# A windowed-attention and gated-FFN stream on one core: another hand-written order for all four engine queues, with other PSUM banks

## The chip, the cores and the metric

The kernel runs on one core of a Trainium2 chip. The metric is the time on the device in microseconds (us). In the rows PE is TensorE, DVE VectorE, ACT ScalarE, POOL GpSimd and SP SyncE; PEld are the weight loads of TensorE, which run beside its matmuls.

## The reference

Eight sequences of 256 tokens and 128 channels. First a layer norm modulated by a small conditioning vector, then causal attention with 8 heads of 128 (stage A), and the same modulation again. Then six layers, each a local attention and a gated FFN, both with a residual. Cut to what matters:

```python
for i in range(6):
    x = attn_layer(shift_tokens(x), Wqkv[i], ...) + x
    x = ffn_layer(shift_tokens(x), ...) + x

def shift_tokens(t):                 # second half of the channels comes from the token before
    a, s = jnp.split(t, 2, -1)
    return concat([a, pad(s, one token in front)[:-1]])

def attn_layer(x):                   # 16 heads of 64
    q, k, v = split(x @ Wqkv)        # 128 -> 3 * 1024
    q, k = l2norm(q) * qs, l2norm(k) * ks
    q, k = rotary(q) * scale, rotary(k) / scale
    sim = q . k * 8, windows of 32 queries on 64 keys, masked
    return softmax(sim) . v @ Wo     # 1024 -> 128

def ffn_layer(x):
    a, gate = split(layernorm(x) @ W1 + b1)      # 128 -> 2 * 341
    return a * gelu(gate) @ W2 + b2              # 341 -> 128
```

## The kernel before

**Work and slots.** A pair of sequences is the unit of the stream: four pairs, six layers, so 24 slots. Slot 0 is in the join (`join_pe`, `join_act`, `join_dve`, `join_pool`), where it overlaps the last sequence of stage A. The other 23 are written once as `pair_pe`, `pair_act`, `pair_dve` and `pair_pool` and called with the layer `l` and the pair `p`. After them `remainder` calls them twice more for the work left (the tail). With `c = 2 * p`, a slot holds three pairs at different ages:

- pair p: sequence c through the local attention up to its values, and the first half of sequence c+1;
- pair p-1: the rest of the attention of sequence c-1, and the output projection of c-2 and c-1;
- pair p-2: its FFN.

The conditions `on(p)`, `on(p - 1)`, `on(p - 2)` switch these off at the ends. In the last slot of a layer (`last(p)`) the projection weights of the next layer are also split into a high and a low part, six times each: the high parts by ACT (`split_high`), the low parts by DVE and POOL (`split_low`).

**The chain of one sequence.** `xt_turn` (PE transposes the input with a column shift), `xt_high` (ACT) and `xt_low` (DVE, L1379), then twelve `proj` (PE, L1428, each three matmuls of 512 columns). Eight of them are queries and keys: `square` (ACT, L1436), `square_sum`, `rotate_cos`, `rotate_sin` (DVE, L1447, L1463, L1468), `rotate_add` (POOL, L1472), nine `norm_step` for all eight, `normalise` (POOL, L1513, writes `qn`), `turn` (PE, four transposes through the helper at L336), `turn_copy` (ACT). Four are values: `move_v` (ACT, L1442). Then `mask` (ACT, writes the mask into a score bank), `scores` (PE, L1555), `row_max`, `less_max` (DVE), `exponent` (ACT, L1577), `row_sum`, `row_inverse` (DVE), `soft_norm` (POOL, L1590, on `sp`), `turn_p` (PE, L336), `copy_p` (ACT, L1608), `values` (PE, L1624), `copy_o` (ACT, L1634), `out_proj` (PE, L1644), `out_add` (DVE).

**The FFN of one pair.** Three transfers on SP's queue (`l_shift`, L1670 to L1683) bring the shifted rows after the pair's last `out_add`. `l_first` (ACT, L1689) copies the unshifted half and waits for their landing; then `l_stats`, `l_moments` (DVE), `l_root` (POOL, four small instructions: L314, L316, L1716, L1718), `l_norm` (ACT), `l_turn` (PE), `l_scale` (ACT), `hidden_gate`, `hidden_a` (PE), `gelu` (ACT), `gated` (DVE), `second_layer` (PE, L1751 to 1791 with `m_add` on DVE).

**What sets the order.** Each engine's queue is written out by hand as a list of calls, and an engine runs its list strictly in order. Every call waits by itself for its inputs. The banks are in constant tables; where a bank is used again, the list has an explicit wait for its last reader in front of the call:

```python
            if on(p - 1):
                e.wait_ge(b_ev.sem, b_ev.at(l * B + c - 1, 2))
                turn(e, l, c - 1, 0)
```

Here `b_ev` counts the value copies `move_v` of a sequence (0 to 3), `b_oc` its `copy_o`, `b_ab` its `rotate_sin`, `b_tc` its `turn_copy`, `b_sub` its `less_max`, `b_pc` its `copy_p`, `b_wx` its `out_add`. In the tables the first list is for even sequences and the second for odd ones. In the names of the rows, `pO`, `pQ` and the like are the eight PSUM banks, `sp` the softmax tiles, `ra`, `rb`, `rs` those of the rotation and the norms.

## Time and profile before

| | |
|---|---|
| median of 3 runs | 1841.77 us (1838.03 to 1850.27) |
| the profiled execution | 1840.85 us |
| its span | 1839.0 us |
| instructions | 65209 |
| PE busy in the span | 1685.9 us |

The span goes from the first instruction to the last; the profiled execution lasts 1.85 us more. Durations below are of this one execution. A matmul's recorded length contains its passage through the array, so consecutive matmuls overlap in the records. Idle time is written in brackets after the instruction that it precedes, with what released it.

### The profile page before, as it was taken

Reading aid. Unit: us, or ns where it says so; the run is one execution under the profiler, and the core shown is the slowest. Engines: PE = TensorE matmul, PEld = TensorE weight load, DVE = VectorE, ACT = ScalarE, POOL = GpSimd, SP = SyncE. Lnnn points to the kernel's source line nnn. Section 1 sums busy time; section 2 is a strip of 40 time slices with the busy share of each in tenths; the row PEclk is TensorE's granted clock in tenths of the full one; section 3 lists DMA queues with packets and bytes.
Section 4 is the critical chain, followed back from the end, with each engine's and each line's share of the span. In section 5 each row is a group of like instructions: output and inputs, shape, how many; then the busy total and the mean of one; then the engine's idle time right before and its main releaser. Section 6 shows DMA issues by size and latency. Waiting matters only on the chain. (4 is left out here: it accounts for less than half of the span.)

```text
span 1839.0 us, 65209 instructions
## 1 busy us (share of the span) xinstructions
PE 1685.9 (92%) x26499; PEld 1384.8 (75%) x26499; DVE 1541.4 (84%) x3101; ACT 1426.3 (78%) x2822; POOL 1395.0 (76%) x1566
## 2 busy tenths in 40 slices
PE   6999976899999999899999899998999989999985
PEld 4788865778778877787787688877877877887773
DVE  5878758788989898899899788988898988888962
ACT  3676764788888888888888788888888878887872
POOL 3777767878878888878787778887787878787850
PEclk9999998999999999999999999999999999999998
DMA  5000010111021201211110212012111111120111
GB/s 165 1 1 2 1 38 21 38 32 48 22 75 50 60 23 38 75 50 40 42 39 28 69 50 59 23 38 75 50 41 42 38 29 42 40 60 28 36 34 29
DMA packets 49368, 76.85 MB, mean 42 GB/s; under 512 B 16316, under 2 KB 29768, under 8 KB 49072
## 3 DMA queue, kind: packets, MB, share of 16 engines
q1 hardware_dynamic: 47600, 70.60, 13.2%
q8 instruction: 212, 3.47, 0.8%
q10 hardware_dynamic: 1472, 2.10, 0.3%
q14 instruction: 84, 0.69, 0.1%
HBM read 21.33 MB, written 1.05 MB: 12 GB/s over the span
## 5 line engine op out<-in xcount | busy, mean ns | idle before, releaser
L1472 POOL TENSOR_TENSOR ra<-ra,rb 128x512 f32<-128x512 f32 x384 | 492.6, 1290 | 89.8 <-DVE rb L1468 89.6
L1513 POOL TENSOR_TENSOR qn<-ra,rs 128x512 f32<-128x512 f32 x384 | 399.6, 1060 | 48.2 <-DVE rs L1506 48.2
L1447 DVE TENSOR_REDUCE ss<-sq 128x8 f32<-128x512 f32 x384 | 259.4, 675 | 71.7 <-ACT sq L1436 67.9
L1590 POOL TENSOR_TENSOR sp<-sp,rl 128x512 f32<-128x512 f32 x192 | 202.1, 1053 | 108.3 <-DVE rl L1585 107.1
L1577 ACT ACTIVATE sp<-sp 128x512 f32<-128x512 f32 x192 | 121.6, 634 | 52.2 <-DVE sp L1572 51.3
L1581 DVE TENSOR_REDUCE sm<-sp 128x8 f32<-128x512 f32 x192 | 128.3, 668 | 5.4 <-ACT sp L1577 5.4
L1608 ACT COPY pt<-pS 64x512 f32<-64x512 f32 x144 | 83.3, 579 | 53.8 <-PE pS L336 52.4
L1555 PE MATMUL pQ<-kT,qT 64*32 64x64 f32 x4608 | 111.3, 226 | 11.6 <-issue 7.7
L1468 DVE TENSOR_TENSOR rb<-pQ,rope 128x512 f32<-128x512 f32 x168 | 114.4, 681 | 1.1
L1463 DVE TENSOR_TENSOR ra<-pQ,rope 128x512 f32<-128x512 f32 x168 | 113.2, 674 | 0.6 <-POOL qn L1513 0.6
L1436 ACT ACTIVATE sq<-pQ 128x512 f32<-128x512 f32 x168 | 100.3, 597 | 15.7 <-PE pQ L1428 11.6
L1555 PEld LDWEIGHTS pQ<-kT,qT 64*32 64x32 f32 x4608 | 94.5, 105 | 18.0 <-issue 16.7
L1608 ACT COPY pt<-pM 64x512 f32<-64x512 f32 x144 | 83.8, 582 | 29.5 <-PE pM L336 28.7
L488 POOL TENSOR_TENSOR ra<-ra,rb 128x512 f32<-128x512 f32 x64 | 81.6, 1291 | 30.0 <-DVE rb L484 30.0
L1644 PE MATMUL pO<-woB,early 128*128 128x128 f32 x768 | 95.7, 278 | 3.3 <-issue 2.4
L1644 PE MATMUL pO<-woB,oT 128*128 128x128 f32 x768 | 95.8, 278 | 3.1 <-issue 3.0
L1644 PEld LDWEIGHTS pO<-woB,oT 128*128 128x128 f32 x768 | 91.8, 194 | 7.8 <-issue 4.5
L1428 PE MATMUL pQ<-w_high,xsh 128*128 128x512 f32 x192 | 92.5, 482 | 2.8 <-issue 2.8
L1644 PEld LDWEIGHTS pO<-woB,early 128*128 128x128 f32 x768 | 91.2, 194 | 3.9 <-issue 2.9
L554 POOL TENSOR_TENSOR sp<-sp,rl 128x128 f32<-128x128 f32 (+1 forms) x128 | 66.8, 545 | 34.8 <-DVE rl L548 34.7
L336 PE MATMUL pS<-eye,qn 128*128 128x128 f32 x480 | 75.7, 281 | 13.1 <-POOL qn L1513 6.1
L1751 PE MATMUL pP<-early,w 128*128 128x512 f32 x144 | 77.8, 622 | 3.1 <-ACT early L1743 2.1
(340 smaller groups left out, 5889.3 us busy)
## 6 DMA issues: line engine op xcount, KB each, us to landing
vs<-v SPq DMA_DIRECT2D x96, 384.0 KB, 3.3
wqkvA<-in_L_ffn_Wqkv SPq DMA_DIRECT2D x18, 512.0 KB, 5.0
vs<-v SPq DMA_DIRECT2D x96, 64.0 KB, 3.0
fx<-xr SPq DMA_DIRECT2D x24, 224.0 KB
woB<-in_L_ffn_Wo SPq DMA_DIRECT2D x6, 512.0 KB, 4.2
w<-in_L_ffn_W SPq DMA_DIRECT2D x6, 341.0 KB, 3.0
out<-x SPq DMA_DIRECT2D x4, 256.0 KB, 2.6
x<-in_L_attn_x SPq DMA_DIRECT2D x1, 768.0 KB, 8.2
```

The lines of the kernel that those rows point to most:

```text
L1436: e.activation(sq[:, j % 2, :], banks[PROJ_BANK[c % 2][n]], ACT.Square).then_inc(b_sq.sem, 1)
L1447: e.tensor_reduce(ss[:, j, :], sq[:, j % 2, :].rearrange("p (h d) -> p h d", d=DB), AX.X, ALU.add).then_inc(b_ss.sem, 1)
L1463: e.tensor_tensor(halves(ra[:, j, :]), r, w, ALU.mult)
L1468: e.tensor_tensor(halves(rb[:, j % 2, :]), r[:, :, ::-1, :], w, ALU.mult).then_inc(b_ab.sem, 1)
L1472: e.tensor_tensor(ra[:, j, :], ra[:, j, :], rb[:, j % 2, :], ALU.add).then_inc(b_ad.sem, 1)
L1513: e.tensor_tensor(qn[:, j % 4, :].rearrange("p (h d) -> p h d", d=DB), ra[:, j, :].rearrange("p (h d) -> p h d", d=DB), rs[:, c % 2, 8 * j ...
L1555: i = e.matmul(o[h][WIN * j:WIN * j + WIN, lo:lo + 2 * WIN], qT[g][r, k, WIN * w:WIN * w + WIN], kT[g][r, k, WIN * w:WIN * w + 2 * WIN], s ...
L1577: e.activation(sp[:, u, :], sp[:, u, :], ACT.Exp, scale=8.0).then_inc(b_ex.sem, 1)
L1581: e.tensor_reduce(sm[:, u, :], groups(sp[:, u, :]), AX.X, ALU.add).then_inc(b_sm.sem, 1)
L1590: e.tensor_tensor(y, y, rl[:, u, :].unsqueeze(2).to_broadcast([P, 8, 64]), ALU.mult).then_inc(b_pn.sem, 1)
L1608: i = e.copy(pt[r, g, u % 2, :, a, :], src[r, :, :])
L1644: i = e.matmul(o[:, t * M:(t + 1) * M], oT[c % 2][:, k, t * P:(t + 1) * P], woB[:, k, :], start=(k == 0), stop=(k == PAIRS - 1))
```

## The change

The four lists of the stream, and the four of the join, get another order, and the bank tables other numbers; the explicit waits in front of the calls follow from these. No call is added or removed, and SP's program, with the shift's transfers, is the same. The order comes from a search in which the shift's transfer was given a later landing. The core of the diff (the first lines are the bank tables; then the join of PE, ACT, DVE and POOL; then the lists of the stream in the same order):

```diff
@@ -50,18 +50,18 @@
...

-PROJ_BANK = [[6, 1, 7, 3, 1, 4, 5, 7, 3, 2, 5, 3], [1, 0, 1, 4, 7, 5, 1, 0, 2, 0, 5, 3]]
-TURN_BANK = [[0, 4, 7, 2, 1, 6, 4, 2], [5, 3, 0, 5, 2, 6, 5, 0]]
-SCORE_BANK = [[0, 2, 3, 2], [4, 0, 5, 0]]
-TURNP_BANK = [[4, 4, 6, 4], [7, 7, 7, 6]]
-VALUE_BANK = [[1, 3, 6, 2], [3, 7, 7, 6]]
+PROJ_BANK = [[4, 3, 2, 7, 1, 4, 3, 0, 2, 5, 3, 5], [0, 7, 1, 2, 7, 5, 6, 0, 4, 3, 2, 4]]
+TURN_BANK = [[6, 2, 4, 0, 6, 1, 1, 2], [4, 5, 1, 6, 4, 3, 5, 6]]
+SCORE_BANK = [[4, 0, 3, 4], [5, 0, 3, 0]]
+TURNP_BANK = [[2, 6, 0, 2], [7, 7, 6, 0]]
+VALUE_BANK = [[6, 1, 0, 6], [2, 7, 6, 1]]
 SCORE_BANKS = range(6)
-XT_FIRST = [2, 7]
-XT_BANK = [6, 7]
+XT_FIRST = [4, 1]
+XT_BANK = [7, 6]
 OUT_BANK = [6, 6]
-LTURN_BANK, Y_BANK = 2, 3
-GATE_BANK = [0, 6, 5]
-A_BANK = [2, 2, 2]
+LTURN_BANK, Y_BANK = 6, 1
+GATE_BANK = [6, 2, 7]
+A_BANK = [5, 6, 6]


 class Tally:
@@ -973,121 +973,121 @@
...
             a_values(e, 7, 2)
+            e.wait_ge(a_ex.sem, a_ex.at(7, 5))
+            xt_turn(e, 0, 0)
...
+            e.wait_ge(a_pc.sem, a_pc.at(7, 6))
+            proj(e, 0, 0, 1)
+            e.wait_ge(a_pj.sem, a_pj.at(7, 2))
             e.wait_ge(a_ex.sem, a_ex.at(7, 7))
...
-            e.wait_ge(a_pc.sem, a_pc.at(7, 6))
             proj(e, 0, 0, 3)
             e.wait_ge(a_pj.sem, a_pj.at(7, 5))
...
+            proj(e, 0, 1, 0)
+            e.wait_ge(b_ab.sem, b_ab.at(0, 3))
+            proj(e, 0, 1, 1)
+            e.wait_ge(a_y.sem, a_y.at(7, 0))
+            turn(e, 0, 0, 0)
             e.wait_ge(b_ab.sem, b_ab.at(0, 6))
-            proj(e, 0, 0, 11)
+            turn(e, 0, 0, 1)
             e.wait_ge(b_ev.sem, b_ev.at(0, 0))
-            proj(e, 0, 1, 0)
-            e.wait_ge(a_pc.sem, a_pc.at(7, 5))
-            turn(e, 0, 0, 0)
-            e.wait_ge(b_ev.sem, b_ev.at(0, 1))
-            turn(e, 0, 0, 1)
-            e.wait_ge(b_tc.sem, b_tc.at(0, 0))
-            proj(e, 0, 1, 1)
-            e.wait_ge(b_ab.sem, b_ab.at(0, 5))
-            turn(e, 0, 0, 2)
-            e.wait_ge(b_ab.sem, b_ab.at(1, 0))
             proj(e, 0, 1, 2)
...
@@ -1104,21 +1104,21 @@
...
+            e.wait_ge(a_pj.sem, a_pj.at(6, 11))
+            xt_high(e, 0, 0)
             a_exp(e, 7, 6)
             a_copy_p(e, 7, 4)
             e.wait_ge(a_ex.sem, a_ex.at(7, 3))
             a_mask(e, 7, 7)
             a_copy_p(e, 7, 5)
-            a_exp(e, 7, 7)
-            a_copy_p(e, 7, 6)
-            e.wait_ge(a_pj.sem, a_pj.at(6, 11))
-            xt_high(e, 0, 0)
-            a_copy_p(e, 7, 7)
             e.wait_ge(a_pj.sem, a_pj.at(7, 11))
             xt_high(e, 0, 1)
...
@@ -1186,19 +1184,16 @@
             a_max(e, 7, 6)
             a_inverse(e, 7, 5)
             a_gates(e, 7)
+            xt_low(e, 0, 0)
             a_inverse(e, 7, 6)
+            xt_low(e, 0, 1)
             a_max(e, 7, 7)
-            a_inverse(e, 7, 7)
-            xt_low(e, 0, 0)
-            a_residual(e, 7)
-            a_stats2(e, 7)
-            xt_low(e, 0, 1)
             square_sum(e, 0, 0, 0)
-            a_norm2(e, 7)
             e.wait_ge(a_tr.sem, a_tr.at(7, 0))
             rotate_cos(e, 0, 0, 0)
             e.wait_ge(a_ad.sem, a_ad.at(7, 6))
             rotate_sin(e, 0, 0, 0)
+            a_inverse(e, 7, 7)
             square_sum(e, 0, 0, 1)
...
@@ -1207,11 +1202,14 @@
             square_sum(e, 0, 0, 2)
             e.wait_ge(a_tr.sem, a_tr.at(7, 2))
             rotate_cos(e, 0, 0, 2)
+            a_residual(e, 7)
             rotate_sin(e, 0, 0, 2)
+            a_stats2(e, 7)
             square_sum(e, 0, 0, 3)
             e.wait_ge(a_tr.sem, a_tr.at(7, 3))
...
             a_soft(e, 7, 6)
+            rotate_add(e, 0, 0, 0)
             a_soft(e, 7, 7)
-            a_root2(e, 7)
-            a_modulate2(e, 7)
-            rotate_add(e, 0, 0, 0)
             rotate_add(e, 0, 0, 1)
             rotate_add(e, 0, 0, 2)
+            a_root2(e, 7)
             rotate_add(e, 0, 0, 3)
+            a_modulate2(e, 7)
             rotate_add(e, 0, 0, 4)
             rotate_add(e, 0, 0, 5)
             norm_step(e, 0, 0, 0)
...
@@ -1805,275 +1799,315 @@
...
             c = 2 * p
             if on(p - 1):
-                e.wait_ge(b_oc.sem, b_oc.at(l * B + c - 2, 2))
+                e.wait_ge(b_ev.sem, b_ev.at(l * B + c - 1, 0))
             if on(p):
                 xt_turn(e, l, c)
             if on(p - 1):
+                e.wait_ge(b_ev.sem, b_ev.at(l * B + c - 1, 3))
+                turn(e, l, c - 1, 0)
+                e.wait_ge(b_oc.sem, b_oc.at(l * B + c - 2, 3))
+            if on(p):
+                xt_turn(e, l, c + 1)
+            if on(p - 1):
+                e.wait_ge(b_ev.sem, b_ev.at(l * B + c - 1, 1))
+                turn(e, l, c - 1, 1)
+                e.wait_ge(b_oc.sem, b_oc.at(l * B + c - 2, 1))
+                turn(e, l, c - 1, 2)
+                e.wait_ge(b_tc.sem, b_tc.at(l * B + c - 1, 0))
+            if on(p):
+                proj(e, l, c, 0)
+            if on(p - 1):
+                e.wait_ge(b_ab.sem, b_ab.at(l * B + c - 1, 7))
+            if on(p):
+                proj(e, l, c, 1)
+            if on(p - 1):
                 e.wait_ge(b_ev.sem, b_ev.at(l * B + c - 1, 2))
-                turn(e, l, c - 1, 0)
-                e.wait_ge(b_ev.sem, b_ev.at(l * B + c - 1, 0))
-            if on(p):
-                xt_turn(e, l, c + 1)
-            if on(p - 1):
-                e.wait_ge(b_ev.sem, b_ev.at(l * B + c - 1, 3))
-                turn(e, l, c - 1, 1)
+            if on(p):
+                proj(e, l, c, 2)
+                e.wait_ge(b_xs.sem, b_xs.at(l * B + c, 0))
+                proj(e, l, c, 3)
+                e.wait_ge(b_xs.sem, b_xs.at(l * B + c + 1, 0))
+            if on(p - 1) and not on(p):
+                e.wait_ge(b_oc.sem, b_oc.at(l * B + c - 2, 3))
+            if on(p - 1):
...
+            if on(p):
+                proj(e, l, c, 4)
+                e.wait_ge(b_ab.sem, b_ab.at(l * B + c, 0))
+            if on(p - 1) and not on(p):
+                e.wait_ge(b_tc.sem, b_tc.at(l * B + c - 1, 0))
+            if on(p - 1):
+                turn(e, l, c - 1, 4)
+                scores(e, l, c - 1, 0)
+            if on(p):
+                e.wait_ge(b_ab.sem, b_ab.at(l * B + c, 1))
+            if on(p - 1) and not on(p):
                 e.wait_ge(b_ab.sem, b_ab.at(l * B + c - 1, 7))
-                turn(e, l, c - 1, 2)
-            if on(p):
-                e.wait_ge(b_xs.sem, b_xs.at(l * B + c, 0))
-                proj(e, l, c, 0)
-            if on(p - 1):
-                e.wait_ge(b_oc.sem, b_oc.at(l * B + c - 2, 0))
-            if on(p):
-                proj(e, l, c, 1)
-            if on(p - 1):
...
+                e.wait_ge(b_wx.sem, b_wx.at(l * B + c - 2, 0))
+            if on(p - 1):
+                turn_p(e, l, c - 1, 2)
+            if on(p):
+                e.wait_ge(b_tc.sem, b_tc.at(l * B + c, 1))
...
+            if on(p - 1) and not on(p):
                 e.wait_ge(b_sub.sem, b_sub.at(l * B + c - 1, 3))
-            if on(p):
...
             if on(p - 2):
                 second_layer(e, l, p - 2, 0)
             if on(p):
-                e.wait_ge(b_pc.sem, b_pc.at(l * B + c, 0))
-                turn_p(e, l, c, 1)
+                scores(e, l, c, 1)
+                e.wait_ge(b_ab.sem, b_ab.at(l * B + c + 1, 4))
+            if on(p - 1) and not on(p) and not on(p):
+                e.wait_ge(b_oc.sem, b_oc.at(l * B + c - 1, 2))
+            if on(p - 1):
+                out_proj(e, l, c - 1, 0)
+                out_proj(e, l, c - 1, 1)
+            if on(p):
+                e.wait_ge(b_tc.sem, b_tc.at(l * B + c, 7))
+                turn_p(e, l, c, 0)
                 e.wait_ge(b_sub.sem, b_sub.at(l * B + c, 3))
                 proj(e, l, c + 1, 8)
-                e.wait_ge(b_ab.sem, b_ab.at(l * B + c + 1, 5))
+                e.wait_ge(b_sub.sem, b_sub.at(l * B + c, 2))
                 proj(e, l, c + 1, 9)
+            if on(p - 1):
+                e.wait_ge(b_wx.sem, b_wx.at(l * B + c - 1, 0))
+            if on(p) and not on(p - 1):
+                e.wait_ge(b_ab.sem, b_ab.at(l * B + c + 1, 4))
+            if on(p):
+                turn_p(e, l, c, 1)
             if on(p - 2):
                 second_layer(e, l, p - 2, 1)
...
@@ -2090,50 +2124,53 @@
...
+            if on(p):
+                square(e, l, c, 1)
+            if on(p - 1):
+                e.wait_ge(b_tc.sem, b_tc.at(l * B + c - 1, 1))
+                mask(e, l, c - 1, 0)
+                e.wait_ge(b_oc.sem, b_oc.at(l * B + c - 2, 2))
                 mask(e, l, c - 1, 1)
-            if on(p):
-                square(e, l, c, 1)
-            if on(p - 1):
                 turn_copy(e, l, c - 1, 3)
...
                 mask(e, l, c, 3)
+                exponent(e, l, c, 1)
                 square(e, l, c + 1, 5)
-                copy_p(e, l, c, 0)
                 exponent(e, l, c, 2)
                 exponent(e, l, c, 3)
             if on(p) and last(p):
                 split_high(e, l + 1, 1, 0)
             if on(p):
                 square(e, l, c + 1, 6)
+                copy_p(e, l, c, 0)
             if on(p) and last(p):
...
                 copy_p(e, l, c, 3)
-                e.wait_ge(b_pc.sem, b_pc.at(l * B + c, 3))
-                mask(e, l, c + 1, 0)
                 copy_o(e, l, c, 0)
                 move_v(e, l, c + 1, 0)
...
         def pair_dve(e, l, p, on):
             c = 2 * p
+            if on(p - 2):
+                l_moments(e, l, p - 2)
             if on(p):
                 xt_low(e, l, c)
                 xt_low(e, l, c + 1)
...
                 norm_step(e, l, c + 1, 8)
             if on(p - 1):
                 l_stats(e, l, p - 1)
-                l_moments(e, l, p - 1)

         def pair_pool(e, l, p, on):
             c = 2 * p
             if on(p - 1):
+                normalise(e, l, c - 1, 0)
+                normalise(e, l, c - 1, 1)
+                normalise(e, l, c - 1, 2)
+                rotate_add(e, l, c - 1, 7)
                 normalise(e, l, c - 1, 3)
             if on(p - 1) and last(p - 1):
                 split_low(e, l + (p - 1) // FP + 1, 1, 2)
+            if on(p - 2):
+                l_root(e, l, p - 2)
             if on(p - 1):
                 normalise(e, l, c - 1, 4)
                 normalise(e, l, c - 1, 5)
-            if on(p - 2):
-                l_root(e, l, p - 2)
+            if on(p):
+                rotate_add(e, l, c, 0)
             if on(p - 1):
...
```

Further moves that the excerpt doesn't show in full. On PE, `proj` (c, 10), (c, 11), (c+1, 0), (c+1, 1), `turn` (c, 0), (c, 1) and `proj` (c+1, 2) now come before `turn_p` (c-1, 2), which before followed `turn` (c, 1) after `proj` (c, 11) and (c+1, 0). `turn` 4 and 5 come before `proj` (c+1, 5), `turn` 6 and 7 before `proj` (c+1, 7), and both gates 0 and 1 before `hidden_a` 0. On DVE `row_max`, `less_max`, `gated`, `out_add` and `row_sum` move by one or two calls, and `split_low` with them; on ACT `split_high` does. On POOL `rotate_add` (c, 7) comes before `normalise` (c, 0) instead of behind `normalise` (c, 3), and `rotate_add` (c+1, 4) before `soft_norm` (c, 0).

## Rows read from the trace of the kernel before

**Rows 1.** busy line of the page: us, share of span, instructions
```profile
PE 1685.9 (92%) x26499; PEld 1384.8 (75%) x26499; DVE 1541.4 (84%) x3101; ACT 1426.3 (78%) x2822; POOL 1395.0 (76%) x1566
```

**Rows 2.** windows, stream and tail: length, busy PE, PEld, DVE, ACT, POOL
```profile
268.28:1768.50 1500.22, 1411.13 (x24501) 1159.78 (x24501) 1328.81 (x2550) 1222.04 (x2262) 1197.35 (x1292) 0.99 0.15 44
1768.50:1839.00 70.50, 43.83 (x570) 30.61 (x568) 20.30 (x39) 28.06 (x47) 15.61 (x19) 0.87 0.09 26
```

**Rows 3.** windows, slot 0, a layer's last, its first, a regular slot
```profile
268.28:327.77 59.49, 41.63 (x533) 32.21 (x533) 44.82 (x87) 31.08 (x59) 39.83 (x44) 0.86 0.09 25
700.67:765.72 65.05, 60.49 (x1045) 49.01 (x1044) 58.54 (x111) 54.64 (x102) 51.92 (x56) 1.00 0.12 35
765.72:827.40 61.68, 59.58 (x1048) 48.89 (x1046) 55.29 (x107) 51.33 (x96) 51.06 (x56) 1.00 0.24 73
1144.10:1204.11 60.01, 59.31 (x1047) 48.80 (x1045) 54.90 (x106) 51.24 (x96) 49.41 (x55) 1.00 0.13 38
```

**Rows 4.** timeline of PE, regular slot: start, length, operation [idle before]
```profile
1141.70 0.39 PE L1428 MATMUL pT<-w_high,xsh 128*128 128x512 f32 x1
...
1142.40 0.38 PE L336 MATMUL pO<-eye,xr 128*128 128x128 f32 x2
1143.03 0.65 PE L336 MATMUL pS<-eye,qn 128*128 128x128 f32 x4 [0.26 <-ACT v L1442]
...
1147.88 0.38 PE L336 MATMUL pP<-eye,qn 128*128 128x128 f32 x2
...
1171.80 0.60 PE L336 MATMUL pQ<-eye,qn 128*128 128x128 f32 x4
1172.23 0.60 PE L336 MATMUL pS<-eye,qn 128*128 128x128 f32 x4
...
1173.09 0.63 PE L336 MATMUL pM<-eye,sp 128*128 128x128 f32 x4 [0.26 <-POOL sp L1590]
```

**Rows 5.** timeline of PE in a slot before it
```profile
911.40 1.50 PE L1644 MATMUL pO<-woB,oT 128*128 128x128 f32 x12 [1.04 <-issue]
```

**Rows 6.** timelines of DVE and ACT, join
```profile
262.22 0.23 DVE L608 COPY gb<-early 128x128 f32<-128x128 f32 x1
...
273.21 0.69 DVE L1447 TENSOR_REDUCE ss<-sq 128x8 f32<-128x512 f32 x1
...
263.31 0.50 ACT L567 COPY early<-pQ 128x384 f32<-128x384 f32 x1
...
267.40 0.74 ACT L1369 CAST xsh<-pP 64x256 fp32r<-64x256 f32 x2 [0.20 <-issue]
```

**Rows 7.** PE groups, stream: count | busy, mean | idle before, releasers
```profile
L336 PE MATMUL pM<-eye,sp 128*128 128x128 f32 x279 | 44.1, 280 | 7.8 <-POOL sp L1590 4.0 <-issue 2.9 <-POOL sp L554 0.9
```

**Rows 8.** timeline of ACT, regular slot, its end
```profile
1189.97 1.17 ACT L1608 COPY pt<-pS 64x512 f32<-64x512 f32 x2 [2.05 <-PE pS L336]
...
1202.83 0.66 ACT L1442 COPY v<-pT 128x512 f32<-128x512 f32 x1
```

**Rows 9.** timeline of POOL, regular slot
```profile
1145.52 3.05 POOL L1513 TENSOR_TENSOR qn<-ra,rs 128x512 f32<-128x512 f32 x3
...
1150.59 1.04 POOL L1513 TENSOR_TENSOR qn<-ra,rs 128x512 f32<-128x512 f32 x1
```

**Rows 10.** timeline of PE, a layer's last slot and the next first
```profile
757.22 0.63 PE L336 MATMUL pS<-eye,sp 128*128 128x128 f32 x4 [0.87 <-POOL sp L1590]
...
771.01 0.63 PE L336 MATMUL pP<-eye,qn 128*128 128x128 f32 x4 [0.91 <-POOL qn L1513]
```

**Rows 11.** tail: timeline of PE, and the chain that ended last
```profile
1803.09 3.14 PE L1644 MATMUL pO<-woB,early 128*128 128x128 f32 x26 [0.88 <-ACT early L1634]
...
1809.13 2.72 DMA fx<-xr
```

**Rows 12.** timelines of SP and ACT, the shift of a regular slot
```profile
1194.37 1.48 SPq L1683 DMA_DIRECT2D fx<-xr  x2
...
1200.61 0.43 ACT L1689 COPY fx<-xr 128x256 f32<-128x256 f32 x1
```

562 lines of the change are left out of this document (281 added, 281 removed).

## The prediction

> **What bounds the kernel now.** I began with the busy line of the page: PE is busy for 92% of the span, DVE 84%, ACT 78%, POOL 76% [rows 1]. Such shares are means over stages, so the next view is the table of stretches [rows 2]: stage A's attention fills the first 268.3 us, then come the stream of 24 slots (1500.2 us) and the tail (70.5 us). Four fifths of the time is the stream. There PE is busy for 1411 of 1500 us, DVE for 1329. A regular slot shows it more sharply [rows 3]: in 60.01 us PE is busy 59.31, DVE 54.90, ACT 51.24, POOL 49.41. The timeline of PE then says what busy means [rows 4]: two turns of four transposes start 0.43 us apart (1171.80, 1172.23) although each is recorded as 0.63 or 0.60 long. So starts, not lengths, measure PE (a projection takes 0.70, from 1141.70 to 1142.40). Counted by starts, the same slot holds some 57 us of work, and PE has real gaps of about 3 us in it. They fall into three kinds: about 1.1 us at the seam between two slots, where turns wait for POOL's normalised rows and for ACT's last value copies; 0.43 us at the third turn_p of sequence c-1; and one stall of 1.0 to 1.3 us in which PE waits for no semaphore, as the 1.04 us of idle put down to "issue" in another slot [rows 5]. An order of instructions can win the first two and not the last. It can win more where the slots are irregular: the last slot of a layer takes 65.05, the first 61.68, slot 0 only 59.49, but with PE busy for just 41.63 of it [rows 3].
>
> The diff adds and removes no instruction and no byte, apart from waits; every engine has the same work. So the sum is over gaps only.
>
> **The change, part by part.**
>
> T1, the join. DVE's first square_sum starts at 273.21 [rows 6]. It needs xt_low of both inputs, and ACT's xt_high is at 267.40 because it stands behind exponents and probability copies. The new order puts both xt_high earlier (the first behind copy 3, the second behind copy 5), and xt_low directly after the gates at 262.22 and the inverse behind them. On ACT the second xt_high then comes out at about 263.8 (after an early copy at 263.31 of 0.50), DVE's second xt_low and one maximum of stage A follow, and square and sum put the first square_sum at about 266.1: 7.1 us earlier. The residual, statistics and norm of stage A are not gone: they now stand between the first rotations, some 1.6 us of DVE, so 5.5 us earlier is what is left. Projection (1,1) no longer waits behind turn (0,0), which may help later on and is not counted. From the other side, PE is busy for 41.6 of 59.5 us here, and whatever ends last further on may eat the lead. Bounds: -9 to -2. Taken: -5.5.
>
> T2, the regular slot, about 21 of 24. Turn_p 2 now comes two projections and two turns later, while soft_norm is only a rotate_add later or not at all. Its wait is 0.86 us between starts (1172.23 to 1173.09) less 0.43, so 0.43 [rows 4]. The group of these instructions idled 4.0 us for POOL's sp in the whole stream [rows 7], about 15 times the 0.26 of this one; slot by slot I count 14 in the 21: -6.0. At the seam, turn 0 now waits for ACT's last value copy instead of the one before. Such a copy is recorded as 0.66 long [rows 8], and turn 0 already waits for one of them, with 0.26 idle [rows 4]; I estimate +0.37 for it. In front of projection 0 the wait for xt_low (0.17) goes, since two turns more stand ahead, and smaller waits at turn 6 and l_turn of 0.1 too. Net +0.1 x 21 = +2. The dangerous piece is on POOL: l_root moves in front of normalise 4 and 5 and takes from 1148.57 to 1150.59, so 2.0 us [rows 9]. Three normalises fill 1145.52 to 1148.57, so normalise 4 ended at 1147.56 and will end at 1149.56. Turn 4 issues at 1147.88 now and stands two projections (0.70 us each, 1.40 together) later, at 1149.28, with the 0.37 of turn 0 at 1149.65. Hidden, with 0.1 us to spare: that is the cover, and if it is gone the cost is up to 2.0 us in each slot. Both ends for the seam: -1.0 to +2.3 per slot. T2 = -4.
>
> The other moves on ACT: mask (c-1,0) goes from the end of one slot to the start of the next (0.4 to 0.5 us), where it lengthens the queue ahead of turn_copy 3 and 4, and shortens it where ACT's last group is late. Exponents 2 and 3 come before copy_p 0, in front of which ACT idled 2.05 us for PE [rows 8]; the idle time is used, but ACT is off the path, so 0. On DVE the moves are by one or two instructions inside runs that never idle long; between -0.2 and +0.2 per slot, 0 taken. POOL's rotate_add 7 before normalise 0 delays the first normalise by 1.3 us, but turn 0 now comes after two projections more, so 0.
>
> T3, the ends of layers. The last slot of a layer has six ACT copies and six subtractions more (54.64 and 58.54 us of ACT and DVE busy against 51.24 and 54.90 [rows 3]), and PE waits in it at many places, once 0.87 us for POOL's sp [rows 10]. Against a regular slot it loses 65.05 - 60.01 = 5.0 us. Exactly such a queue gains from another order, and as easily loses: these copies are moved too, three between squares. The first slot of a layer loses 1.7 against the regular one and idles 0.91 for one normalised row [rows 10], since split_low 2 (1.28 us) stands on POOL there, and now l_root stands behind it, ahead of normalise 4. I take -0.8 for each of five last slots and +0.7 for each of five first: -0.5, with +-7.5.
>
> T4, the tail of 70.5 us, a chain with PE busy for 43.83 [rows 2]. Second_layer 0 can fill the 0.88 us in front of the last out_proj [rows 11]; l_root stands ahead of a turn here too and costs up to its 2.0 us if PE is waiting. +0.4 taken, -1 to +2 as bounds.
>
> T5, the shift. Its three transfers are issued after out_add: the last two from 1194.37, ending at 1195.85 [rows 12]. The transfer of the same shift in the tail's chain is 2.72 us [rows 11], so it lands at about 1198.6, and l_first, ACT's last call, runs at 1200.61. That is 2.0 us of slack. SP's program is unchanged, and in the new order out_add of c-1 comes at most 1 us later, since both halves of out_proj go behind the scores. Cost 0 in the regular slot, at most 1 us elsewhere. A planner that knew of a later landing therefore gains nothing here; it moves l_moments into the next slot's list, where DVE would meet it at the same place in the cycle.
>
> Sum: -5.5 - 4 - 0.5 + 0.4 = -9.6 us. On the profiled run's 1840.85 (span plus 1.85) this is 1831.2; the median of the runs stands 0.92 higher, so the forecast is 1832.
>
> **The rivals.** B, slower: l_root ahead of normalise 4 with turn 0's later release. Price: turn 0's 0.37 is not regained and turn 4 waits for its row; it decides where PE reaches turn 4 before normalise 4 ends, 0.1 us away by my reckoning. At 1.2 us a slot (half of 0.37 + 1.97) over 23 slots it gives +27.6, with the join's -5.5: 1841.8 + 22 = 1864; at the full 2.34 it gives +48 and 1890. For it: the margin is small and POOL would carry it to each later turn. Against: POOL has 10 us of idle per slot [rows 3]. C, more gain: the last slots lose only half of their 5 us (-12.5), the seam gains 1.0 in 14 slots (-14) and the join 9: -35.5, 1806. For it: the gaps are there. Against: in a regular slot three waits of 0.2 to 0.3 us each would all have to go. D, nothing: PE's starts are back to back, whatever is won at one place is waited for at the next, and the join's lead ends at DVE (44.82 of 59.49 busy) or PE before slot 1 begins: 1842 +-3. E, PE is not the bound: a slot has 48.80 us of weight loads in 60.01 [rows 3], 81%, so PE would have headroom and DVE with 54.90 would set the pace: 5.1 x 21 = 107 us to gain, 1735. The Trainium skill, "Perfetto Trace Analysis", Identifying the Most-Contended Engine, says that busy time of matmuls is no good measure and weight-load share is. The trace contradicts the consequence: by starts PE has only about 3 us of gaps in the slot, so I give this almost nothing.
>
> **How the numbers follow.** Forecast A, 1832 with 1824 to 1842 as its own range: 0.44. B 0.12, C 0.21, D 0.21, E 0.02. One per cent, 18.4 us, is about what a measurement of this kernel can tell from no change (its three runs span 12.2): the bounds are 1823.4 and 1860.2. Faster by more: nearly all of C, all of E and a small part of A, 0.27. Slower: two thirds of B and a little from the last and first slots together with the tail, 0.10. The rest is 0.63. The range may leave out 2 in 10: it reaches down to C's time, 1806, leaving out E and half of C, and up to 1858, leaving out two thirds of B.
>
> **What the profile after would show.** T1: first square_sum near 266 to 268 and slot 0's start to slot 1's start not longer than 59.5 by more than the lead. T2: no wait for sp at turn_p 2, slots of 59.8; turn 4 with no wait for qn. If B holds, turn 4 shows idle put down to POOL's qn in most slots. T3: last slots under 65. T5: l_first without idle put down to a DMA. The prediction is wrong if the gaps at last slots close together (then faster by over 1%), or if POOL's queue is late at the seam (then slower).

## The result, and the profile after

| | before | after |
|---|---|---|
| median of the runs | 1843.01 us (4 runs) | 1870.72 us (4 runs) |
| lowest and highest | 1838.03 to 1850.27 | 1862.95 to 1875.64 |
| ratio of the two | | 1.0155, interval 1.0127 to 1.0183 |
| profiled execution, its span | 1840.85, 1839.0 us | 1862.95, 1861.2 us |
| mean granted clock of TensorE | 0.984 | 0.974 |

The new order is 1.55% slower, where 1832 us was forecast; it lies outside the range, and on the other side. The profiled execution of after is the fastest of its four, so its trace shows 22 us of the 28 us.

The busy line of the page after, against [rows 1]: PE is busy for 4.6 us more in a span that is 22 us longer. So most of the time is idle time of PE.

```profile
PE 1690.5 (91%) x26499; PEld 1408.7 (76%) x26499; DVE 1532.5 (82%) x3101; ACT 1419.7 (76%) x2822; POOL 1390.4 (75%) x1566
```

The stretches that answer to [rows 2] and the first of [rows 3] (length, busy PE, PEld, DVE, ACT and POOL with their counts; then the granted clock, DMA's share and GB/s): slot 0, the rest of the stream, the tail.

```profile
262.00:325.00 63.00, 44.46 (x550) 34.72 (x547) 48.84 (x96) 33.30 (x69) 42.08 (x49) 0.81 0.13 42
325.00:1780.00 1455.00, 1367.30 (x23941) 1145.54 (x23942) 1270.05 (x2453) 1182.33 (x2199) 1150.89 (x1246) 0.99 0.15 44
1780.00:1862.00 82.00, 51.16 (x613) 36.58 (x609) 23.37 (x50) 31.51 (x55) 17.73 (x21) 0.79 0.10 28
```

**Where the time came from, by place.** A slot is measured from the first transpose of its input to the next slot's. Slot 0 begins 6.0 us earlier (260.91 for 266.88). It is 3.9 longer and slot 1 3.7 shorter, so that behind these two after leads by 5.8. Slots 2 to 22 are 19.0 us longer together, slot 23 is 2.1 longer, and from the last projection to the end it takes 78.7 us for 71.9. The sum, -5.8 + 19.0 + 2.1 + 6.8 = +22.1, is the difference of the spans. The 19.0 us aren't spread evenly: slots 2, 5, 8, 11, 14, 17 and 20 are 20.4 us longer together, the other fourteen 1.3 shorter.

**By cause.** First the groups of `scores` on PE, between 262 and 1800 us, in before (count | busy, mean ns | idle before, with releasers):

```profile
L1555 PE MATMUL pQ<-kT,qT 64*32 64x64 f32 x4608 | 111.3, 226 | 11.6 <-issue 7.7 <-ACT pP L1537 3.7
L1555 PE MATMUL pS<-kT,qT 64*32 64x64 f32 x3072 | 73.4, 227 | 7.6 <-issue 7.6
L1555 PE MATMUL pP<-kT,qT 64*32 64x64 f32 x3072 | 73.3, 226 | 2.5 <-issue 2.5
```

and in after:

```profile
L1549 PE MATMUL pS<-kT,qT 64*32 64x64 f32 x4608 | 113.3, 227 | 24.4 <-issue 22.5 <-ACT pQ L1531 1.8
L1549 PE MATMUL pQ<-kT,qT 64*32 64x64 f32 x4544 | 110.7, 227 | 13.7 <-issue 13.7
L1549 PE MATMUL pT<-kT,qT 64*32 64x64 f32 x3008 | 71.5, 225 | 5.5 <-issue 4.2 <-ACT pS L1531 1.3
```

Each matmul is as long as before. "Issue", idle time with no semaphore behind it, has gone from 17.8 us in these three groups (19.8 with a fourth, on `pT`) to 40.4. Call by call, taking each step of more than 0.3 us between two matmuls of one `scores` call: before has 21 such stalls, 23.8 us together; after has 31, 46.5 us. Most of the new time sits in one of the four calls of a slot: `scores` (c, 1) has 20.8 us for 2.2. There they are 2.0 to 2.5 us each, in slot 0 and then in every third slot (2, 5, 8 and so on to 23).

Those are the slots that grew. Taken slot by slot, what the stalls inside `scores` gained or lost is what the slot gained or lost, within 1.3 us in 20 of the 21 slots 2 to 22: in all they grew by 21.6 us there, and the slots by 19.0. The one slot that got much shorter, slot 12 by 4.6 us, had a stall of 3.5 us in `scores` (c-1, 0) before and none in this execution of after.

One of the stalls of `scores` (c, 1), in the timeline of PE. It stands four fifths of the way through the call, which began at 1188.11; behind it comes the first `out_proj`.

```profile
1188.11 0.24 PE L1549 MATMUL pT<-kT,qT 64*32 64x64 f32 x1
...
1191.58 0.21 PE L1549 MATMUL pS<-kT,qT 64*32 64x64 f32 x1 [2.16 <-issue]
...
1191.93 4.80 PE L1638 MATMUL pO<-woB,early 128*128 128x128 f32 x26
```

Such a stall may cost more than itself. After four of the seven stalls of `scores` (c, 1) in slots 2 to 20 the clock falls. In the windows of the same slot the granted clock is 0.50 from 1193.10 to 1196.30, the 1.2 GHz level; PE has then been idle for 2.16 us and worked again for 1.5. In that stretch the steps of `out_proj` are 0.214 us apart, in the others 0.112. (That the stall brings the fall is not shown: after the other three the clock stayed at 1.00.) Before, the same part of a regular slot has 1.00 throughout (second fence).

```profile
1182.00:1191.58 9.58, 7.42 (x268) 6.58 (x252) 6.76 (x12) 6.66 (x14) 6.99 (x7) 1.00 0.18 51
1191.58:1193.10 1.52, 1.52 (x32) 1.43 (x32) 1.03 (x3) 0.00 (x0) 0.16 (x1) 0.99 0.06 11
1193.10:1196.30 3.20, 3.20 (x17) 3.20 (x17) 2.77 (x5) 1.26 (x2) 0.88 (x1) 0.50 0.00 0
1196.30:1204.00 7.70, 7.70 (x105) 7.26 (x106) 5.86 (x12) 5.31 (x10) 5.17 (x9) 0.99 0.12 34
```

```profile
1182.00:1191.00 9.00, 9.00 (x185) 8.14 (x184) 8.67 (x17) 6.83 (x13) 7.46 (x7) 1.00 0.20 55
1191.00:1194.00 3.00, 3.00 (x24) 2.83 (x23) 3.00 (x7) 1.62 (x4) 1.58 (x2) 1.00 0.00 0
```

The other causes in slots 2 to 22 nearly cancel. In the view of waits, the matmuls of PE idle for POOL 9.2 us where before has 19.7, for ACT 19.3 where before has 7.4 (12.6 of it in front of `turn` (c-1, 0), most of the rest in last slots, where `values` waits for the copied probabilities), and for DVE 5.3 for 7.2. By the spacing of PE's starts the gap in front of `turn` (c-1, 0) at the seam rises from 9.4 to 16.0 us. The time at a granted clock of 0.50 rises from 6.8 to 17.1 us; at half speed that can cost at most 5 us more. The seam, and the wait that is left on POOL (timeline of PE; the seam of a regular slot, then `turn` 4 of a layer's first slot, which answers to the second of [rows 10]):

```profile
1144.46 0.38 PE L336 MATMUL pM<-eye,xr 128*128 128x128 f32 x2
1145.29 0.66 PE L336 MATMUL pS<-eye,qn 128*128 128x128 f32 x4 [0.46 <-ACT v L1436]
...
1151.07 0.63 PE L336 MATMUL pS<-eye,qn 128*128 128x128 f32 x4
```

```profile
774.21 0.63 PE L336 MATMUL pS<-eye,qn 128*128 128x128 f32 x4 [1.82 <-POOL qn L1507]
```

In the regular slot `turn` 4, at 1151.07, has no wait at all. In a layer's first slot it has one of 1.82 us.

### The profile page after: what moved, and what is told of

It reads as the page before. It is cut to its first block and busy times, and to the rows that moved or that the text cites. A ratio compares the mean times of both kernels' runs of the same rounds, so it can differ in the third digit from the quotient of the medians.

```text
span 1861.2 us, 65211 instructions
## 1 busy us (share of the span) xinstructions
PE 1690.5 (91%) x26499; PEld 1408.7 (76%) x26499; DVE 1532.5 (82%) x3101; ACT 1419.7 (76%) x2822; POOL 1390.4 (75%) x1566
## 3 DMA queue, kind: packets, MB, share of 16 engines
q8 instruction: 212, 3.47, 0.8%
## 5 line engine op out<-in xcount | busy, mean ns | idle before, releaser
L1584 POOL TENSOR_TENSOR sp<-sp,rl 128x512 f32<-128x512 f32 x192 | 198.6, 1043 | 177.0 <-DVE rl L1579 176.9
L1549 PE MATMUL pS<-kT,qT 64*32 64x64 f32 x4608 | 113.3, 227 | 24.4 <-issue 22.5
L1549 PEld LDWEIGHTS pS<-kT,qT 64*32 64x32 f32 x4608 | 95.7, 106 | 32.5 <-issue 30.9
L1560 DVE TENSOR_REDUCE mx<-pS 128x8 f32<-128x512 f32 x72 | 49.4, 686 | 60.6 <-PE pQ L1549 60.6
L336 PE MATMUL pS<-eye,qn 128*128 128x128 f32 x480 | 74.7, 279 | 25.6 <-ACT v L1436 14.2
L336 PEld LDWEIGHTS pS<-eye,qn 128*128 128x128 f32 x480 | 55.7, 142 | 47.5 <-ACT v L1436 20.1
L1618 PE MATMUL pO<-pt,vs 128*64 128x64 f32 x1152 | 74.4, 226 | 10.8 <-DVE early L1773 5.6
L1745 PE MATMUL pO<-early,w 128*128 128x512 f32 x144 | 78.8, 630 | 4.8 <-ACT pt L1602 1.7
L1422 PE MATMUL pS<-w_high,xsh 128*128 128x512 f32 x168 | 75.5, 450 | 7.8 <-DVE rb L1462 4.2
```

Source lines behind the costliest of these rows:

```text
L336: return e.matmul(o[:, n * P:(n + 1) * P], y, ident, is_transpose=True, start=(n == 0), stop=True, skip_group_check=True)
L1422: i = e.matmul(o, x_[:, c % 2, t * P:(t + 1) * P], w[:, kind, g * CH:(g + 1) * CH], start=(k == 0), stop=(k == 2))
L1549: i = e.matmul(o[h][WIN * j:WIN * j + WIN, lo:lo + 2 * WIN], qT[g][r, k, WIN * w:WIN * w + WIN], kT[g][r, k, WIN * w:WIN * w + 2 * WIN], s ...
L1584: e.tensor_tensor(y, y, rl[:, u, :].unsqueeze(2).to_broadcast([P, 8, 64]), ALU.mult).then_inc(b_pn.sem, 1)
L1745: e.matmul(banks[bank_][0:k, :], w1[:, half * F + n * P:half * F + n * P + k], xnT, start=True, stop=True)\
```

## What the experiments had to tell apart

What the trace shows of the instructions themselves: the page lists a DMA queue of kind "instruction" with 212 packets and 3.47 MB, the same in both kernels.

```profile
q8 instruction: 212, 3.47, 0.8%
```

That is 16.4 KB a packet, and 212 packets for the some 54,300 instructions of PE's queue are one for every 256 of them. The Trainium skill says the same of its size ("Advanced Engine Details and Errata", ISA Cache: lines of 16 KB, 256 instructions) and, in "Runtime: NRT & Kernel Launch", Instruction fetch mechanics, that the next block is fetched while the current one executes and that the cost is mostly hidden. The first agrees with the 16.4 KB. The second holds at most of the 212 boundaries, but at 43 of them in after, and 35 in before, PE steps by 0.3 us or more at a boundary, 2.0 to 3.2 us after the start of a block's transfer.

Counted from the records of the trace, all stalls inside `scores` fall at one and the same place modulo 256, number 193 or 194, in every kernel. I take this for the boundary of two blocks. The 1.04 us of [rows 5] stands there too, 2.7 us after the start of a block's transfer.

One `scores` call is 128 matmuls and 128 weight loads: 256 instructions in 1.4 us when nothing stalls, so it uses up a whole block in that time. From the start of a block's transfer, one packet, to PE's going on after a long stall it is 2.2 to 2.7 us. In most places the transfer starts about 1.1 us after PE has gone into the block ahead; ahead of the stalls of `scores` (c, 1) it starts 2.3 to 5.1 us after (crossing at 1185.12, transfer from 1188.89, PE goes on at 1191.58). At the corresponding block of before the crossing is at 1184.29, the transfer starts at 1185.81, and there is no stall. In the block of after PE had 4.1 us of work besides the stall, so by these numbers a transfer started after 1.1 us would have landed in time.

So the theory (F in the expectations): what stalls PE is the delivery of its own instructions, and the order decides it, because it puts `scores` (c, 1), 256 quick instructions, behind other calls than before. In before the first half of `out_proj` stands directly ahead of it and the second behind it; in after both stand behind it, and the larger transfer of `move_values` (on SP's queue: it writes the values, shifted by a window, into `vs`; 458,752 bytes) is issued 4.9 us ahead of it instead of 6.5. Rivals: the stalls come with any code and the 28 us are waits (the seam, POOL's l_root); it is only where the calls happen to fall in the blocks of 256; it is the traffic of `move_values`.

## The experiments

**1. The traffic taken away.** After, with the transfer of the second half of the values cut down to one row from the second layer on (most of the shifted values that the windows need are then left out).

```diff
-            e.dma_start(vs[g][WIN:P, :, :], v[g][0:P - WIN, :, :]).then_inc(b_vs[g].sem, 16)
+            top = WIN + 1 if g == 1 and l > 0 else P
+            e.dma_start(vs[g][WIN:top, :, :], v[g][0:top - WIN, :, :]).then_inc(b_vs[g].sem, 16)
```

> The changed kernel, but from the second layer on the large transfer of move_values for the second half of the heads (458,752 bytes in all for one call, behind the last value products of sequence c-1) moves one partition row instead of 96. Its output is therefore not the reference's; every instruction and wait stays. Theory F (code fetch): in the changed kernel PE's code block for scores (c,1) is requested while this transfer is in flight, and comes 3 to 5 us after the line before was entered, so PE stands for 2.0 to 2.5 us inside scores (c,1) in one slot of three, with nothing to wait for. With the transfer gone those stalls fall below 1 us: 7 x 1.5 = 10 us, and 5 to 8 us of low clock behind them, so 1850 to 1858. Rival S (semaphores: the added time is waits at the seam and at the gated tiles): no change, 1868 to 1873. Rival G (code fetch, but limited only by its own latency and not by the traffic): the stalls stay at 2.0 to 2.5 us, no change.

Measured: 1869.82 us (1864.56 to 1876.04), ratio to before 1.0169 (1.0133 to 1.0205). The stalls of `scores` (c, 1) are 20.5 us, all stalls in `scores` 51.4. That is after's own time: this traffic is not the cause of the stalls in (c, 1). (The experiments ran on other chips than the first two kernels. Before was run beside them, with medians of 1840.2 to 1843.4 us; after was not, so a difference to after is one of medians across chips.)

The 4.9 us more of stalls are one stall of 5.9 us, in `scores` (c-1, 0) of slot 12. The traces of experiments 3 and 4 have it too, with 5.9 and 7.3 us, and before with 3.5; the profiled execution of after, the fastest of its four, has none. It may be a good part of what that trace lacks against the median. Other traffic is in flight there: the weights and scales of the next layer, some 1.7 MB on SP's queue. In the trace of experiment 4 (timelines of SP and PE):

```profile
1026.92 1.30 SPq L2581 DMA_DIRECT2D wqkvA<-in_L_ffn_Wqkv  x3
...
1039.28 0.31 PE L1549 MATMUL pS<-kT,qT 64*32 64x64 f32 x1 [6.99 <-issue]
```

PE had gone into the block ahead at 1026.23, and the next block's transfer started only at 1036.85. Whether the weights hold it up was not tested.

**2. Another place in the blocks.** After, with 52 stand-alone semaphore increments on PE ahead of its stream, so that every later call begins 52 instructions further on in its block.

```diff
+            for _ in range(52):
+                e.sem_inc(e_hold.sem, 1)
```

> The changed kernel with 52 PE instructions that only raise a counter nobody reads, at the start while PE waits for its first data. They shift all later PE code by 52 instructions against the blocks of 256 in which it is fetched. Theory F: the scores calls that stall are those which begin 200 to 265 instructions into a block; the shift takes most of those of scores (c,1), scores (c-1,0) and part of scores (c,0) out of that window, so the stalls of scores (c,1) fall from seven to one or two, and the time falls by 12 to 25 us, to 1846 to 1859. Rival S (only the order of waits matters): within 3 us of the changed kernel, 1868 to 1873.

Measured: 1888.26 us (1886.71 to 1891.79), ratio 1.0270 (1.0241 to 1.0300), so 18 us more than after and outside both expectations. About 3 us of it is the increments' own delay, since slot 0 begins at 264.09 for 260.91. The stalls rise from 46.5 to 55.4 us, those of (c, 1) from 20.8 to 26.3, and the time at the low clock behind 262 us from 78 to 101. The expected sign was wrong: the shift took some calls out of bad places and brought as many others in. That the stalls moved at all shows that the place in the block matters. The groups of `scores` on PE:

```profile
L1549 PE MATMUL pS<-kT,qT 64*32 64x64 f32 x4544 | 114.0, 226 | 33.4 <-issue 31.6 <-ACT pQ L1531 1.8
L1549 PE MATMUL pQ<-kT,qT 64*32 64x64 f32 x4480 | 109.7, 226 | 6.3 <-issue 6.3
L1549 PE MATMUL pT<-kT,qT 64*32 64x64 f32 x3008 | 72.5, 226 | 12.2 <-issue 10.9 <-ACT pS L1531 1.3
```

By number modulo 256, with the boundary at 194, the stalls of (c, 1) of 2 us and more come in both traces when the call begins at 196 or later, or up to 24, so within some 90 instructions behind a boundary; at 26 to 40 they are 0.8 to 1.0 us, and from 44 to 189 there are none. A slot moves the place by some 86 instructions, which is a third of 256: hence every third slot.

**3. The order of before at that one call.** After, with `out_proj` (c-1, 0) ahead of `scores` (c, 1), with its waits.

```diff
             if on(p):
-                scores(e, l, c, 1)
                 e.wait_ge(b_ab.sem, b_ab.at(l * B + c + 1, 4))
...
             if on(p - 1):
                 out_proj(e, l, c - 1, 0)
+            if on(p):
+                scores(e, l, c, 1)
+            if on(p - 1):
                 out_proj(e, l, c - 1, 1)
```

> The changed kernel with out_proj (c-1,0) ahead of scores (c,1) again, as before the change. Its bank's wait (rotate_sin (c+1,4), ending about 0.4 us after the call's turn comes) moves with it. Theory F: scores (c,1) comes 1.8 us later behind the transfer of move_values and behind scores (c,0), the stalls in it fall from 2.2 to about 0.4 us in seven slots, -12 us and -5 us of low clock, +0.4 x 22 = +9 us for the wait: 1858 to 1867. Rival S: only the +9, 1875 to 1882.

Measured: 1893.10 us (1886.91 to 1903.29; the trace is of the slowest), ratio 1.0300 (1.0256 to 1.0343), outside both expectations. The stalls of `scores` (c, 1) are gone but for slot 0: 2.6 us for 20.8. But the kernel is 22 us slower. The later scores make DVE's chain late, and behind 262 us PE's matmuls idle for DVE 45.2 us, in after 15.3. Most of it is in these two groups of PE:

```profile
L1638 PE MATMUL pO<-woB,early 128*128 128x128 f32 x736 | 94.3, 281 | 10.7 <-DVE rb L1462 8.7 <-issue 1.8
L1422 PE MATMUL pS<-w_high,xsh 128*128 128x512 f32 x168 | 76.5, 455 | 26.5 <-DVE sp L1566 21.9 <-DVE rb L1462 4.0 <-DVE xsl L1373 0.6
```

The call begins at the same places here (247, 254, 5) as it does where after stalls (244, 251, 253), and goes through. What stands ahead of the dense call decides its stall there; and the order of after is built around the early scores, so one call can't be put back alone.

**4. The seam.** After, with the second input transpose ahead of `turn` (c-1, 0), so that it fills the wait for ACT's value copy.

```diff
-                e.wait_ge(b_ev.sem, b_ev.at(l * B + c - 1, 3))
-                turn(e, l, c - 1, 0)
...
                 xt_turn(e, l, c + 1)
             if on(p - 1):
+                e.wait_ge(b_ev.sem, b_ev.at(l * B + c - 1, 3))
+                turn(e, l, c - 1, 0)
```

> The changed kernel with the second input transpose (0.22 us) ahead of turn (c-1,0) instead of behind it; the turn waits for ACT's last value copy anyway, the input transpose only for an output copy that is some 0.7 us older. Rival S and my own term for the seam (turn 0 waits 0.3 to 0.4 us longer than before the change, in each of 22 slots): the 0.22 us fill idle time, -0.22 x 22 = -5 us, 1864 to 1868. Theory F has nothing to say on it, but if all of the added time were code fetch the seam would show no idle to fill and the time would stay within 2 us.

Measured: 1878.72 us (1875.21 to 1880.58), ratio 1.0219 (1.0186 to 1.0253), 8 us slower than after, where 2 to 7 us of gain were expected. The gap at the seam went from 16.0 to 11.4 us, as reckoned; nothing of it reached the end. The stalls in `scores` (c-1, 0) rose from 12.0 to 19.7 us, and the low clock from 78 to 91. Nearly all of the rise is the stall of 7.3 us in slot 12, told under experiment 1, which experiment 1 has with after's own order of PE. So the rise can't be put down to this edit. In the trace slot 12 is 8.5 us longer than in after's, of 12.2 us in all.

**5. The shift in before.** Before with 40 such increments: an order that has `out_proj` ahead of `scores` (c, 1), with other places in the blocks.

```diff
+            for _ in range(40):
+                e.sem_inc(e_hold.sem, 1)
```

> The kernel before, with 40 PE instructions that only raise a counter nobody reads, at its start (0.15 us each, in the time in which PE waits for its first data). Theory F (blocks of 256 instructions): in the kernel before, scores (c,1) never begins 196 to 228 instructions into a block in the stream, and never stalls; the shift of 40 brings it there in some five slots. If the place in the block decides, those five stall by about 2.2 us each, 8 to 11 us in all, and the time rises by 8 to 15 us, to 1848 to 1856. Rival O (the order of calls ahead of scores (c,1) decides, and out_proj ahead of it protects it at every place): scores (c,1) stays without stalls, the time within 4 us of the kernel before.

Measured: 1855.38 us (1844.33 to 1868.01, ten runs) for 1843.37 (23 runs), ratio 1.0064 (1.0040 to 1.0088). In the trace, `scores` (c, 1) begins at 199, 206, 213, 215 and 222 in five slots, where the order of after stalls (experiment 2 at 196, 203, 210, 212 and 219), and stalls in one of them only. At 13, 20 and 27 it doesn't stall either, where experiment 2 has 2.2 to 2.5 us at 10, 17 and 24. The trace of before shows the same without any edit: it begins the call at 229, 236, 243, 245, 252, 3, 10 and 12 with no stall, where after, at 228 to 253, has 2.1 to 2.5 us each time. So at that call the order ahead decides. The time, though, came out where the other theory had put it: the mere place of the code costs some 12 us in the median, in an unchanged order. The trace is of the fastest run and shows no more than 29.0 us of stalls for 23.8, so where these 12 us are isn't shown.

**6. POOL's l_root put back.** After, with l_root behind normalise 5, as in before.

```diff
-            if on(p - 2):
-                l_root(e, l, p - 2)
             if on(p - 1):
                 normalise(e, l, c - 1, 4)
                 normalise(e, l, c - 1, 5)
+            if on(p - 2):
+                l_root(e, l, p - 2)
```

> The changed kernel with l_root behind normalise 4 and 5 again on POOL. In the changed kernel turn (c-1,4) waits 1.9 us for its row in the first slot of each layer, 9.6 us in five slots, and not in regular ones. If l_root's 2.0 us ahead of it is the cause, that wait goes in the first slots, and what is late next is turn 5 or the layer norm's turn, which now comes 2 us later: between -9 and 0 us, taken -5, so 1862 to 1870. My rival B of the prediction (l_root costs in every slot): -20 us or more.

Measured: 1859.74 us (1851.33 to 1864.52), ratio 1.0079 (1.0049 to 1.0108), 11 us faster than after. In the groups of PE the waits of `turn` for the normalised rows are down from 11.3 us to 0.4, and `l_turn` now waits for the FFN's norm instead, 6.8 us where after has none:

```profile
L336 PE MATMUL pS<-eye,qn 128*128 128x128 f32 x480 | 74.0, 277 | 15.0 <-ACT v L1436 14.2 <-POOL qn L1507 0.4 <-issue 0.3
L336 PE MATMUL pO<-eye,early 128*128 128x128 f32 x92 | 14.4, 281 | 6.9 <-ACT early L1719 6.8
```

The same two groups in after:

```profile
L336 PE MATMUL pS<-eye,qn 128*128 128x128 f32 x480 | 74.7, 279 | 25.6 <-ACT v L1436 14.2 <-POOL qn L1507 11.3
L336 PE MATMUL pO<-eye,early 128*128 128x128 f32 x92 | 14.2, 279 | 0.0
```

That is 4 us at first hand. The rest of the 11 isn't located; the two profiled executions differ by 3.4 us only. The stalls of `scores` are what they were, 46.3 us for 46.5, and the kernel is still 16 us slower than before.

**7. The same seam edit in before.** `xt_turn` (c+1) ahead of `turn` (c-1, 0).

```diff
-                e.wait_ge(b_ev.sem, b_ev.at(l * B + c - 1, 2))
-                turn(e, l, c - 1, 0)
...
                 xt_turn(e, l, c + 1)
             if on(p - 1):
+                e.wait_ge(b_ev.sem, b_ev.at(l * B + c - 1, 2))
+                turn(e, l, c - 1, 0)
```

> The kernel before with the second input transpose ahead of turn (c-1,0). PE idles about 0.4 us by starts there in most slots, and 0.22 us of it can be filled: -0.22 x 20 = -4.4 us, 1835 to 1839. In the changed kernel the same edit took 4.6 us from this wait but the time did not fall; if what is won at the seam is waited for again elsewhere, the time stays within 2 us here too.

Measured: 1843.01 us (12 runs) for 1843.37 (23 runs), ratio 0.9993 (0.9981 to 1.0005): no difference. The stalls are 27.0 us for 23.8.

**8 and 9. The dense call cut in half, in after and in before.** `scores` (c, 1) does 64 of its 128 matmuls (half of these scores are left out). If its length against a block makes the stall, after must gain more than before.

```diff
-            for k in range(4):
+            for k in range(2 if g == 1 and c % 2 == 0 else 4):
```

> The changed kernel with scores (c,1) of even sequences cut to the first 64 of its 128 matmuls; the rest of those scores is left out, so the output is not the reference's. All waits and all other calls stay. The work left out is 0.7 us in 24 slots, 17 us at most. Theory F (the dense block of scores (c,1) uses up its code faster than the next block of code comes, 2.0 to 2.5 us in one slot of three): these stalls go too, 19.7 us, and some 5 us of low clock behind them, so 1870 - 17 - 25 = 1828 to 1836, and the distance to the same edit of the kernel before falls from 28 us to 0 to 10. Rival S (semaphore waits): only the 17 us or less, 1853 to 1860, and the distance stays at 25 to 30.

> The kernel before with the same edit: scores (c,1) of even sequences cut to 64 of 128 matmuls, the rest of those scores left out. It stalls there only once (slot 0, 2.1 us), so by either theory it wins the 0.7 us in 24 slots where PE has no semaphore wait behind it, 10 to 17 us: 1825 to 1833.

Measured: after 1839.16 us (1825.79 to 1845.38, ten runs), ratio to before 0.9985 (0.9964 to 1.0007); before 1826.62 (1826.16 to 1829.99), ratio 0.9929 (0.9910 to 0.9947). The cut takes 31.6 us from after's median (29 if each is set against before on its own chip) and 14.0 from before's (1840.63 on this chip). The stalls of (c, 1) are 0 in both. The groups of `scores` in after with the cut:

```profile
L1549 PE MATMUL pQ<-kT,qT 64*32 64x64 f32 x4608 | 114.0, 231 | 8.1 <-issue 8.1
L1549 PE MATMUL pS<-kT,qT 64*32 64x64 f32 x3840 | 97.9, 232 | 13.1 <-issue 11.2 <-ACT pQ L1531 1.8
L1549 PE MATMUL pT<-kT,qT 64*32 64x64 f32 x2304 | 56.3, 225 | 3.1 <-issue 1.8 <-ACT pS L1531 1.3
```

Issue has gone from 40.4 us to 21.1. The distance of the two orders falls from 27.7 us of the medians to 12.5 (of the profiled executions, from 22.1 to 11.6). So some 15 of the 28 us go with the second half of that one call. This is no clean measure of its stalls: the cut also takes 128 instructions out of every slot and so moves all later calls in their blocks. What is left holds stalls at the same place too. Counted over all calls of PE, by steps of 0.3 us and more at a boundary, the two orders have 38.7 and 59.2 us uncut, and 30.6 and 36.8 with the cut: 20.5 us apart, then 6.2. The time at the low clock behind 262 us doesn't fall with it in after (77.6 us with the cut and without it; before 49.7, with the cut 40.1): most of it is in the join and the tail, so the slower clock belongs to what is left.

No version here that does all the work beats the kernel before.

## Why the prediction was wrong, by its own steps

**The step that failed** is in its first part: "An order of instructions can win the first two and not the last", the last being the stall with "issue" behind it. It had seen one of 1.04 us [rows 5], took it for a constant of 1.0 to 1.3 us a slot, and put no term for it into the sum. It is no constant. Already in before the stalls in `scores` are 21 of 0.3 to 3.5 us, in 12 of the 24 slots and in the tail, and the regular slot of [rows 3] has none. Its length depends on which calls stand ahead of a dense one (experiments 3 and 5), on where the calls fall in the blocks of 256 instructions (experiment 2), and on how long the dense call is (8 and 9). The change made these stalls 22.7 us longer, and in slots 2 to 23 they grew by 23.7 us where the slots grew by 21.2. By the cut calls they are at least about half of the 28 us; the sum had 0. Without them the stream would have come out near its forecast: the slots 2 to 22 less their stalls are 2.4 us shorter, for which T2 and T3 had -4.5.

**T1, the join, -5.5.** The number is right, -5.8 with slots 0 and 1, and the first `square_sum` starts at 267.5, 5.7 us earlier, where 7.1 was reckoned. How it got there was partly luck: slot 0 lost 3.9 us again, and of the 3.7 that slot 1 won, 1.4 is a shorter stall in its `scores` (c-1, 1).

**T2, regular slots, -4.** The wait at the third `turn_p` (6.0 us of gain) is gone: no group of PE waits for `sp` of L1584 between 262 and 1800, where before had 11.5 us of such waits. The later release of `turn` 0, +0.37 a slot, measured +0.31. The dangerous piece, l_root ahead of normalise 4, hides in regular slots as reckoned, by a margin of 0.1 us that held: `turn` 4 has no wait. So the parts in waits were right, and the slots still grew: the ones that are neither a layer's first nor its last by 14.6 us, just as much as their stalls.

**T3, ends of layers, -0.5 with +-7.5.** In the first slots `turn` 4 waits about 1.9 us in each of the five, 9.6 us, where the forecast had +3.5 for the five. Little of it comes out in the slots: they are 2.4 us longer together, 0.8 without their stalls. The last slots are 2.1 us longer, but their stalls grew by 5.3, so without them they won 3.2, for a forecast of -4. Putting l_root back gives 11 us (experiment 6), of which 4 are accounted for. The place was named; its price is not settled.

**T4, the tail, +0.4 with -1 to +2.** Measured +6.8. The waits for normalised rows behind l_root are there, two of 2.04 and 2.13 us (timeline of PE):

```profile
1786.78 0.92 PE L336 MATMUL pO<-eye,qn 128*128 128x128 f32 x4 [2.04 <-POOL qn L1507]
...
1789.83 1.08 PE L336 MATMUL pS<-eye,qn 128*128 128x128 f32 x4 [2.13 <-POOL qn L1507]
```

Before has one of 2.04 and one of 0.75 at this point, so they are 1.4 us of the 6.8. Another part is likely the clock, of which the forecast had no term: 0.79 and then 0.67 in the next stretches, and 0.75 over the last 47 us, where before has 0.93 and 0.84 (second fence). Behind the last projection after is at the low clock for 33.2 us, before for 19.0. What that costs is not shown. An estimate from experiment 5, whose tail keeps the order of before: 10.4 us more at the low clock there go with 2.3 us more of tail besides the stalls, so 14.2 would be some 3 us.

```profile
1780.00:1792.00 12.00, 7.11 (x142) 5.50 (x141) 4.33 (x12) 7.32 (x16) 11.20 (x13) 0.79 0.27 79
1792.00:1800.00 8.00, 7.18 (x85) 4.58 (x68) 3.56 (x6) 5.62 (x10) 1.73 (x2) 0.67 0.00 0
...
1815.00:1862.00 47.00, 25.28 (x167) 17.23 (x166) 8.63 (x19) 9.65 (x16) 1.72 (x4) 0.75 0.10 28
```

```profile
1766.00:1790.00 24.00, 17.78 (x333) 12.56 (x332) 9.28 (x20) 16.04 (x30) 13.76 (x15) 0.93 0.14 41
1790.00:1839.00 49.00, 28.06 (x251) 19.41 (x249) 13.23 (x28) 14.25 (x23) 4.35 (x6) 0.84 0.10 27
```

**T5, the shift, 0.** Right: in the stream no `l_first` is held up by a transfer; the one in the tail waits 10.0 us for it, in before 9.1, and the planner's later landing shows nowhere.

**The rivals.** B gave 1864 for slower and came nearest, but for the most part by another cause: its wait shows in first slots and in the tail only, and undoing it gives back 11 us, not 27. D (nothing reaches the end) and C fell. E fell too: what PE loses in its queue comes out in the length of the slots, and DVE, with 82% of the span, follows.

**What stays open.** Some 12 of the 28 us are left when the dense call is cut. The stalls in other calls, the tail (+6.8), l_root and the seam lie in them, the join's -5.8 against them; their shares can't be told apart to a microsecond, since an edit of a few instructions moves the medians by 0 to some 15 us through the places of the code alone. What makes the transfer of a block start up to 5 us late ahead of `scores` (c, 1), and some 10 us late in slot 12, is not known. For (c, 1) it is not the larger transfer of `move_values`; for slot 12 the weights in flight are an untested candidate.

## What to carry to other kernels

In a PE queue of small matmuls, idle time that the trace puts down to issue is a cost of the order like any wait: find out at which instruction number it falls, and if that number repeats modulo 256, do not put a call of 256 quick instructions behind other quick ones; keep slow matmuls (here `out_proj`) ahead of it, if the engines that wait for the call can bear the delay; in experiment 3 they couldn't. A planner that prices only waits and engine times doesn't see this, nor the slower clock that can follow such a stall. And an experiment on such a kernel needs a control that only shifts the code, or a few per mille of gain or loss say nothing of the edit.
